# Layer norm of a Macaron pair of blocks: GpSimd's power of minus one half in two instructions of two tiles each, and VectorE's four centring instructions in two pairs

## The chip, the cores and the metric

The kernel runs on one core of a Trainium2 chip. The metric is the device time of one execution in microseconds (us), the median of several runs; lower is better. Engines are called as in the profile: PE is TensorE's matmul side and PEld its weight load, DVE is VectorE, ACT is ScalarE, POOL is GpSimd, SP is SyncE, which here only issues DMAs.

## What is computed

Eight batches of 512 tokens by 128 features go through two blocks. The first ("A") is a low-rank feed-forward, causal attention with 16 heads, and the feed-forward again; the second ("B") is a mixture of experts, linear attention with a Taylor feature map, and the mixture again. A layer norm stands ahead of each of these six, and one more inside the attention of block A.

```
def _layernorm(x, axis=-1, eps=1e-05):
    m = jnp.mean(x, axis=axis, keepdims=True)
    v = jnp.var(x, axis=axis, keepdims=True)
    return (x - m) / jnp.sqrt(v + eps)
...
    x = x + 0.5 * _L0_ffn_ref(_layernorm(x, axis=-1), L0_ffn_U1, L0_ffn_V1, L0_ffn_b1, L0_ffn_U2, L0_ffn_V2, L0_ffn_b2)
    x = x + _L0_attn_ref(_layernorm(x, axis=-1), L0_attn_Wq, L0_attn_Wk, L0_attn_Wv, L0_attn_Wo, L0_attn_gamma, L0_attn_beta)
...
    x = x + _L1_attn_ref(_layernorm(x, axis=-1), L1_attn_Wq, L1_attn_Wk, L1_attn_Wv, L1_attn_Wo)
```

That is seven layer norms for each of eight batches, 56 in all, and each is over 512 tokens: four tiles of 128 tokens (one token a partition) by 128 features.

## The kernel before

**Streams.** Two streams run side by side. In the steady part the "left" one works through block A of batch i+1 (A1) while the "right" one works through block B of batch i (B2). Each has its own half of SBUF and four PSUM banks. The tables `ORDER_A` and `ORDER_B` list the steps of a block, and strings of L and R in `LOOP` say, for each engine by itself, from which stream its next step comes. The order on every engine is thus fixed by hand: an engine whose next instruction has to wait does nothing else meanwhile. There are a beginning, a body of five turns, and a finish.

**One layer norm.** It is three steps on four engines:

- `stat` on DVE: four `bn_stats` (L879) and four `bn_aggr` (L882), one a tile, leave mean and variance in `h.mv`, and the last one raises `mv_ready`.
- `stat` on POOL (`ln_scale`, L678): it adds epsilon to the four variances (L680, 128x4), waits for that through `vare_ready`, and raises them to the power of minus one half (L682, 128x4, the exponents in `neghalf`) into `h.rstd`, which raises `rstd_ready`.
- `centre` on DVE (L885): it waits for `rstd_ready`, and four `tensor_scalar` (L890), one a tile of 128x128, subtract the mean and multiply by `rstd`. The last one raises `ln_ready`.
- `norm` or `split` on PE (L1140): it waits for `ln_ready` and transposes the four tiles (L1145) into one bank, which ACT reads out next (L731 or L735).

Between its `stat` and its `centre` DVE may have steps of the other stream, as its string has it; where it has none, it waits for POOL.

**What else POOL does.** It masks: `affine_select` (L689) on the attention weights of either stream, and for block B a `tensor_scalar` over 128x1024 or 128x512 (L709) that adds one. These are POOL's other steps, and they stand in its order between those of the layer norms.

Of the kernel before, what the change touches and what calls it, by code (L numbers as in the profile page):

```python
# [33 lines left out]
ALU = mybir.AluOpType  # L34
# [5 lines left out]
NT = S // P  # L40
# [29 lines left out]
def segment(kt, head, heads):  # L70


    if kt == 0:
        return head * S
    if kt == 1:
        return (heads + head) * S
    if kt == 3:
        return (heads + head) * S + WIDTH[1]
    return 2 * heads * S + head * WIDTH[2]
# [301 lines left out]
def build_program(nc, x, w, cst, out):  # L381
    ctx = ExitStack()
    with ctx:  # L383
        def sb(name, shape, dt=F32):
            return ctx.enter_context(nc.sbuf_tensor(name, shape, dt))
# [16 lines left out]
        neghalf = sb("neghalf", [P, NT])  # L402
# [150 lines left out]
        def run(eng, fns, engine):  # L553

            steps(fns, 0, "begin", engine)
            for i in range(TURNS):
                steps(fns, i, "body", engine)
            steps(fns, 0, "finish", engine)
# [15 lines left out]
        def drained(h, it, step, unit):  # L574

            u = h.T[step, unit]
            return it * (h.per.act if u.engine == "act" else h.per.dve) + u.count
# [86 lines left out]
        @block.gpsimd  # L664
        def _(pool):
            for h in (A1, A2):
                pool.memset(h.vaug[:, :, :, HD0:HD0 + 1], 1.0).then_inc(setup, 1)
            pool.memset(neghalf[:, :], -0.5).then_inc(setup, 1)
            pool.memset(epsilon[:, :], LN_EPS).then_inc(setup, 1)
            for k in range(GP):  # L670
                if k:
                    pool.memset(column[:, k, 0:k], 0.0)
                pool.memset(column[:, k, k + 1:32], 0.0)
                last = pool.memset(column[:, k, k:k + 1], 1.0)
            last.then_inc(setup, 1)
            pool.wait_ge(setup, SETUP)

            def ln_scale(h, it, k, step):  # L678
                pool.wait_ge(h.mv_ready, it * h.lns + k + 1)
                pool.tensor_tensor(h.vare[:, :], h.mv[:, :, 1], epsilon[:, :], ALU.add).then_inc(h.vare_ready, 1)  # L680
                pool.wait_ge(h.vare_ready, it * h.lns + k + 1)
                pool.tensor_tensor(h.rstd[:, :], h.vare[:, :], neghalf[:, :], ALU.pow).then_inc(h.rstd_ready, 1)  # L682

            def mask(buf, heads, kt, fill=0.0):

                step = {0: S, 1: S, 3: S, 2: WIDTH[2]}[kt]
                s0 = segment(kt, 0, heads)
                v = bass.AP(buf.tensor, buf.offset + s0, [list(buf.ap[0]), [step, heads], [1, P]])
                return pool.affine_select(out=v, in_=v, compare_op=ALU.is_ge, fill=fill, base=0,  # L689
                                          pattern=[[0, heads], [1, P]], channel_multiplier=-1)  # L690

            def exp(h, it, n, step):
                g, u = divmod(n, NU0)
                if u in COMPLETE0:
                    pool.wait_ge(h.act, drained(h, it, step, "s"))
                for kt in COMPLETE0.get(u, ()):
                    mask(h.probs[:, g % 2, :], GH, kt).then_inc(h.masked0, 1)

            def sq(h, it, n, step):
                p, u = divmod(n, NU1)  # L700
                if u in COMPLETE1:
                    k = p * NC + list(COMPLETE1).index(u)
                    pool.wait_ge(h.act, drained(h, it, step, "s"))
                    for kt in COMPLETE1[u]:
                        last = mask(h.wts[:, p % 2, :], 2, kt, -1.0)
                    last.then_inc(h.cut1, 1)
                    pool.wait_ge(h.cut1, it * NPAIR * NC + k + 1)
                    v = h.wts[:, p % 2, (u // 2 * 2) * S:(u + 1) * S]
                    pool.tensor_scalar(v, v, 1.0, 1.0, ALU.mult, ALU.add).then_inc(h.masked1, 1)  # L709

            run(pool, dict(stat=ln_scale, exp=exp, sq=sq), "pool")


# [118 lines left out]
        def _(dve):  # L832
            passed = Passed(dve)
# [51 lines left out]
            def centre(h, it, k, step):  # L885

                src = h.attn if h in (A1, A2) and k == 2 else h.x
                passed.wait_ge(h.rstd_ready, it * h.lns + k + 1)
                for t in range(NT):
                    last = dve.tensor_scalar(h.ln[:, t, :], src[:, t, :], h.mv[:, t, 0:1], h.rstd[:, t:t + 1],  # L890
                                             ALU.subtract, ALU.mult)
                last.then_inc(h.ln_ready, 1)
# [219 lines left out]
            def out1(h, it, n, step):  # L1112
                ps = full(passed, h, it, step, "y")
                if n:
                    passed.wait_ge(h.dve, drained(h, it, f"out1 {n - 1}", "y"))
                dve.tensor_tensor(h.x[:, :, :].rearrange("p t d -> p (t d)"), ps[:, :],
                                  h.x[:, :, :].rearrange("p t d -> p (t d)"), ALU.add).then_inc(h.dve, 1)

            fns = dict(stat=stat, centre=centre, split=split, low=low, down0=down0, qkv0=qkv0, pad0=pad0, pv0=pv0, turn=turn,
                       out0=out0, take=take, route=route, gate=gate, expert=expert, qk1=qk1, pad1=pad1, recip=recip,  # L1120
                       scale=scale, out1=out1)
# [304 lines left out]
```

## Time and profile before

| | |
|---|---|
| median of 3 runs | 1490.75 us (1488.5 to 1492.01) |
| the profiled execution | 1486.09 us |
| its span, first to last instruction | 1484.4 us |
| mean granted TensorE clock | 0.934 of full speed |
| busy share of the span: PE, DVE, ACT, POOL | 84%, 64%, 49%, 28% |
| a turn of the body | 181 us |
| layer norms: left, right | 31, 25 |

The busy shares say which engine has least room, not what the end waits for. With an order fixed by hand, what counts for an instruction is what ended the idle time before it ("idle before <- releaser"), and whether the engine behind it stood idle for it in turn.

### The profile page before, as it was taken

Reading aid. Unit: us, or ns where it says so; the run is one execution under the profiler, and the core shown is the slowest. Engines: PE = TensorE matmul, PEld = TensorE weight load, DVE = VectorE, ACT = ScalarE, POOL = GpSimd, SP = SyncE. Lnnn points to the kernel's source line nnn. Section 1 sums busy time; section 2 is a strip of 40 time slices with the busy share of each in tenths; the row PEclk is TensorE's granted clock in tenths of the full one; section 3 lists DMA queues with packets and bytes.
Section 4 is the critical chain, followed back from the end, with each engine's and each line's share of the span. In section 5 each row is a group of like instructions: output and inputs, shape, how many; then the busy total and the mean of one; then the engine's idle time right before and its main releaser. Section 6 shows DMA issues by size and latency. Waiting matters only on the chain. (4 is left out here: it accounts for less than half of the span.)

```text
span 1484.4 us, 26633 instructions
## 1 busy us (share of the span) xinstructions
PE 1242.9 (84%) x10064; PEld 705.9 (48%) x10064; DVE 950.1 (64%) x2923; ACT 725.7 (49%) x1247; POOL 417.7 (28%) x707
## 2 busy tenths in 40 slices
PE   5698668987789887899878887798878998879998
PEld 3354234444544455444554445544455445543456
DVE  6985377446974469834797347964488646874267
ACT  3165335643366433664346543465435663456533
POOL 1023101640026400264003540035300362016730
PEclk9699779998999989999999999899998999999999
DMA  3100001000010000100001000010010100011000
GB/s 117 43 2 2 8 22 34 11 8 7 23 44 2 8 13 17 44 1 9 19 11 44 1 9 22 8 44 2 8 29 1 44 2 1 13 38 44 2 2 15
DMA packets 37201, 28.75 MB, mean 19 GB/s; under 512 B 7960, under 2 KB 36304, under 8 KB 37072
## 3 DMA queue, kind: packets, MB, share of 16 engines
q1 hardware_dynamic: 37072, 27.04, 6.7%
q8 instruction: 80, 1.31, 0.4%
q14 instruction: 49, 0.40, 0.1%
HBM read 5.90 MB, written 2.10 MB: 5 GB/s over the span
## 5 line engine op out<-in xcount | busy, mean ns | idle before, releaser
L775 ACT ACTIVATE left<-bank 128x512 f32<-128x512 f32 x280 | 159.9, 598 | 86.3 <-PE bank L1237 84.5
L968 DVE TENSOR_REDUCE left<-bank 128x4 f32<-128x512 f32 x280 | 184.5, 682 | 22.6 <-PE bank L1218 21.8
L819 ACT ACTIVATE right<-bank 128x512 f32<-128x512 f32 x280 | 158.6, 598 | 82.2 <-PE bank L1324 80.1
L689 POOL TENSOR_SCALAR_AFFINE_SELECT left<-left 128x512 f32<-128x512 f32 (+1 forms) x144 | 82.5, 587 | 397.6 <-ACT left L775 382.7
L1160 PE MATMUL bank<-right,pairs 128*128 128x512 f16 x588 | 161.6, 399 | 17.3 <-DVE right L1047 10.1
L1216 PE MATMUL bank<-left 128*128 128x512 f16 (+1 forms) x448 | 123.3, 324 | 42.4 <-DVE left L968 25.9
L709 POOL TENSOR_SCALAR right<-right 128x1024 f32<-128x1024 f32 x168 | 151.9, 904 | 14.7
L689 POOL TENSOR_SCALAR_AFFINE_SELECT right<-right 128x256 f32<-128x256 f32 (+1 forms) x240 | 99.3, 426 | 133.3 <-ACT right L819 122.8
L1350 PE MATMUL bank<-right 128*32 128x256 f32 (+3 forms) x1792 | 134.6, 439 | 0.0
L1068 DVE SCALAR_TENSOR_TENSOR right<-bank,right 128x128 f32<-128x128 f32 x448 | 125.8, 343 | 11.7 <-PE bank L1300 6.4
L1300 PEld LDWEIGHTS bank<-ew,right 128*128 128x128 f32 x896 | 113.8, 191 | 25.8 <-DVE right L1057 12.5
L1300 PE MATMUL bank<-ew,right 128*128 128x128 f32 x896 | 121.0, 278 | 6.0 <-DVE right L1057 5.8
L1237 PE MATMUL bank<-left 128*128 128x512 f16 (+1 forms) x448 | 102.4, 303 | 22.1 <-DVE left L968 13.0
L794 ACT ACTIVATE right<-bank 128x512 f32<-128x512 f32 x112 | 66.2, 597 | 106.5 <-PE bank L1160 105.4
L1218 PE MATMUL bank<-negmask,identb 128*128 128x128 bf16 x512 | 103.5, 234 | 0.0
L1324 PE MATMUL bank<-right 96*128 96x512 f16 x448 | 96.9, 304 | 4.9 <-ACT right L819 1.9
L680 POOL TENSOR_TENSOR right<-right,epsilon 128x4 f32<-128x4 f32 x25 | 5.3, 213 | 332.6 <-DVE right L882 332.6
L1160 PEld LDWEIGHTS bank<-right,pairs 128*128 128x128 f16 x588 | 52.8, 101 | 78.7 <-DVE right L1047 18.0
L1350 PEld LDWEIGHTS bank<-right 128*32 128x32 f32 x1792 | 54.4, 110 | 65.7 <-issue 62.5
L1216 PEld LDWEIGHTS bank<-left 128*128 128x128 f16 x448 | 46.2, 103 | 81.8 <-DVE left L968 30.6
L1337 PE MATMUL bank<-right,column 128*32 128x256 f32 (+3 forms) x896 | 75.7, 447 | 1.2 <-POOL right L709 1.1
L985 DVE COPY left<-bank 128x512 f32<-128x512 f32 x28 | 19.4, 691 | 87.8 <-PE bank L1248 87.8
(274 smaller groups left out, 2201.8 us busy)
## 6 DMA issues: line engine op xcount, KB each, us to landing
right<-right SPq DMA_DIRECT2D x168, 64.0 KB, 2.0
left<-left SPq DMA_DIRECT2D x168, 32.0 KB, 1.8
left<-x_dram SPq DMA_DIRECT2D x7, 256.0 KB, 2.6
out_dram<-right SPq DMA_DIRECT2D x7, 256.0 KB, 2.2
left<-left SPq DMA_DIRECT2D x24, 64.0 KB, 2.0
right<-right SPq DMA_DIRECT2D x24, 32.0 KB, 1.9
wo<-wo_dram SPq DMA_DIRECT2D x1, 512.0 KB, 3.7
ew<-ew_dram SPq DMA_DIRECT2D x1, 512.0 KB, 4.6
```

What stands on the lines that cost most here:

```text
L689: return pool.affine_select(out=v, in_=v, compare_op=ALU.is_ge, fill=fill, base=0, pattern=[[0, heads], [1, P]], channel_multiplier=-1)
L709: pool.tensor_scalar(v, v, 1.0, 1.0, ALU.mult, ALU.add).then_inc(h.masked1, 1)
L775: act.activation(h.probs[:, g % 2, u * S:(u + 1) * S], ps[:, :], ACT.Exp).then_inc(h.act, 1)
L819: act.activation(h.wts[:, p % 2, u * S:(u + 1) * S], ps[:, :], ACT.Square, bias=1.0, scale=FEAT ** -0.5).then_inc(h.act, 1)
L968: dve.tensor_reduce(h.bmax[:, u * NT:(u + 1) * NT], ps[:, :].rearrange("p (b k) -> p b k", k=P), AX.X, ALU.max).then_inc(h.dve, 1)
L1068: last = dve.scalar_tensor_tensor(out=dst[:, t, :], in0=ps[:, t * P:(t + 1) * P], scalar=h.comb[:, t, e:e + 1], in1=h.acc[:, t, :], op0=AL ...
L1160: done = mm(out, left, right, start=first, stop=last)
L1216: mm(ps[:, c0:c0 + n_keys], h.q0a[:, g, qt * P:(qt + 1) * P], h.kpad0[:, g * GH + j, 0:n_keys], start=True, stop=False)
L1218: last = mm(ps[:, c0 + n_keys - P:c0 + n_keys], identb[:, :], negmask[:, :], start=False, stop=True)
L1237: last = mm(ps[:, c0:c0 + WIDTH[kt]], h.kpad0[:, g * GH + j, kt * P:(kt + 1) * P], h.q0a[:, g, kt * P:S], start=True, stop=True)
L1300: last = mm(ps[:, t * P:(t + 1) * P], h.hexp[:, e % 2, t * P:(t + 1) * P], ew2[:, e, :], start=True, stop=True)
L1350: last = mm(h.num[HD1 * j + c:HD1 * j + c + 32, kt * P:S], h.v1[:, kt, hd * HD1 + c:hd * HD1 + c + 32], h.wts[:, p % 2, c0:c0 + WIDTH[kt]] ...
```

## The change

POOL's one power instruction over four columns becomes two over two columns each, and each raises `rstd_ready`, which now counts two for a layer norm. On DVE the wait for `rstd_ready` moves inside the loop: the first two tiles wait for the first power, and the other two for the second. What is computed stays the same, and so do all tables of the order.

```
@@ ln_scale, POOL
                 pool.wait_ge(h.vare_ready, it * h.lns + k + 1)
-                pool.tensor_tensor(h.rstd[:, :], h.vare[:, :], neghalf[:, :], ALU.pow).then_inc(h.rstd_ready, 1)
+                for t in range(0, NT, 2):
+                    pool.tensor_tensor(h.rstd[:, t:t + 2], h.vare[:, t:t + 2], neghalf[:, t:t + 2], ALU.pow)\
+                        .then_inc(h.rstd_ready, 1)
@@ centre, DVE
                 src = h.attn if h in (A1, A2) and k == 2 else h.x
-                passed.wait_ge(h.rstd_ready, it * h.lns + k + 1)
                 for t in range(NT):
+                    passed.wait_ge(h.rstd_ready, (it * h.lns + k) * 2 + t // 2 + 1)
                     last = dve.tensor_scalar(h.ln[:, t, :], src[:, t, :], h.mv[:, t, 0:1], h.rstd[:, t:t + 1],
                                              ALU.subtract, ALU.mult)
                 last.then_inc(h.ln_ready, 1)
```

On POOL, in a turn of the body, at the fourth layer norm of block A (left), with block B's masks (right) behind it, before:

```order
L680 TENSOR_TENSOR left<-left,epsilon 128x4 [waits mv_ready_A1]
L682 TENSOR_TENSOR left<-left,neghalf 128x4 [waits vare_ready_A1]
L689 AFFINE_SELECT right<-right 128x2x128 [waits act_B2]
L709 TENSOR_SCALAR right<-right 128x1024 [waits cut1_B2]
L689 AFFINE_SELECT right<-right 128x2x128 [waits act_B2]
```

and after, with every line number behind L682 higher by two:

```order
L680 TENSOR_TENSOR left<-left,epsilon 128x4 [waits mv_ready_A1]
L683 TENSOR_TENSOR left<-left,neghalf 128x2 [waits vare_ready_A1]
L683 TENSOR_TENSOR left<-left,neghalf 128x2
L691 AFFINE_SELECT right<-right 128x2x128 [waits act_B2]
L711 TENSOR_SCALAR right<-right 128x1024 [waits cut1_B2]
```

The second power stands between the first and the masks, and waits for nothing.

On DVE, in a turn of the body, at the last layer norm of block B (right), which ends in `centre` right behind its own `stat`, before:

```order
L882 BN_AGGR right<-right 128x2 [waits dve_step_B2]
L882 BN_AGGR right<-right 128x2 x3
L890 TENSOR_SCALAR right<-right 128x128 [waits rstd_ready_B2]
L890 TENSOR_SCALAR right<-right 128x128 x3
L919 SCALAR_TENSOR_TENSOR left<-bank1,left 128x512 [waits filled_A1]
```

and after:

```order
L884 BN_AGGR right<-right 128x2 [waits dve_step_B2]
L884 BN_AGGR right<-right 128x2 x3
L892 TENSOR_SCALAR right<-right 128x128 [waits rstd_ready_B2]
L892 TENSOR_SCALAR right<-right 128x128
L892 TENSOR_SCALAR right<-right 128x128 [waits rstd_ready_B2]
L892 TENSOR_SCALAR right<-right 128x128
L921 SCALAR_TENSOR_TENSOR left<-bank1,left 128x512 [waits filled_A1]
```

The third centring instruction has a wait of its own; nothing has changed places.

## Rows read from the trace of the kernel before

**Rows 1.** The page: busy time, share of the span and instructions of each engine.
```profile
PE 1242.9 (84%) x10064; PEld 705.9 (48%) x10064; DVE 950.1 (64%) x2923; ACT 725.7 (49%) x1247; POOL 417.7 (28%) x707
```

**Rows 2.** Waits of the whole span: us in total, times, longest us.
```profile
PEld bank L1145 <- DVE left L890: 39.8, 27, 6.1
...
PEld bank L1145 <- DVE right L890: 31.6, 22, 4.6
...
DVE left L890 <- POOL left L682: 20.8, 18, 2.7
...
DVE right L890 <- POOL right L682: 14.2, 16, 1.4
```

**Rows 3.** POOL's groups by shape: times, busy us, mean ns of one, idle before.
```profile
L689 POOL TENSOR_SCALAR_AFFINE_SELECT right<-right 128x256 f32<-128x256 f32 x224 | 89.3, 410 | 122.9 <-ACT right L819 122.8
L689 POOL TENSOR_SCALAR_AFFINE_SELECT left<-left 128x512 f32<-128x512 f32 x112 | 69.7, 637 | 382.8 <-ACT left L775 382.7
...
L682 POOL TENSOR_TENSOR left<-left,neghalf 128x4 f32<-128x4 f32 x31 | 31.3, 1009 | 2.4
L682 POOL TENSOR_TENSOR right<-right,neghalf 128x4 f32<-128x4 f32 x25 | 25.2, 1008 | 2.0
...
L680 POOL TENSOR_TENSOR left<-left,epsilon 128x4 f32<-128x4 f32 x31 | 6.2, 199 | 153.1 <-DVE left L882 153.1
```

**Rows 4.** Timeline of POOL and DVE (start us, us), right layer norm at 529 us.
```profile
529.05 0.20 POOL L680 TENSOR_TENSOR right<-right,epsilon 128x4 f32<-128x4 f32 x1 [13.64 <-DVE right L882]
529.33 1.01 POOL L682 TENSOR_TENSOR right<-right,neghalf 128x4 f32<-128x4 f32 x1
...
530.38 1.11 DVE L890 TENSOR_SCALAR right<-right 128x128 f32<-128x128 f32 x4 [1.40 <-POOL right L682]
...
531.55 1.12 PE L1145 MATMUL bank<-ident,right 128*128 128x128 f32 x4 [0.36 <-DVE right L890]
```

**Rows 5.** Timeline of POOL and DVE, left layer norm at 491 us, with masks behind.
```profile
491.27 1.01 POOL L682 TENSOR_TENSOR left<-left,neghalf 128x4 f32<-128x4 f32 x1
492.25 0.41 POOL L689 TENSOR_SCALAR_AFFINE_SELECT right<-right 128x256 f32<-128x256 f32 x1
492.75 1.04 POOL L709 TENSOR_SCALAR right<-right 128x1024 f32<-128x1024 f32 x1
...
492.32 2.27 DVE L890 TENSOR_SCALAR left<-left 128x128 f32<-128x128 f32 x4 [0.22 <-POOL left L682]
```

**Rows 6.** Timeline of POOL and DVE: two powers and what DVE ran beside them.
```profile
296.85 1.01 POOL L682 TENSOR_TENSOR left<-left,neghalf 128x4 f32<-128x4 f32 x1
...
297.12 0.18 DVE L1097 COPY dlateB<-right 64x48 f32<-64x48 f32 x1
...
1111.84 1.01 POOL L682 TENSOR_TENSOR right<-right,neghalf 128x4 f32<-128x4 f32 x1
...
1111.88 1.14 DVE L958 TENSOR_SCALAR left<-left,headmask 96x512 f16<-96x512 f16 x4
```

**Rows 7.** Timeline of DVE and PE, right layer norm at 567 us.
```profile
567.86 1.01 POOL L682 TENSOR_TENSOR right<-right,neghalf 128x4 f32<-128x4 f32 x1
...
569.19 1.11 DVE L890 TENSOR_SCALAR right<-right 128x128 f32<-128x128 f32 x4
...
570.36 0.90 PE L1145 MATMUL bank<-ident,right 128*128 128x128 f32 x3 [1.40 <-DVE right L890]
```

**Rows 8.** Two lines' instructions (min/median/max ns), and who waited for L709.
```profile
L890 DVE TENSOR_SCALAR right<-right x100: 334/341/1061, 11.9 to 1456.8; 128x128 f32<-128x128 f32 x100
...
L1097 DVE COPY dlateB<-right x14: 183/183/516, 297.1 to 1442.2; 64x48 f32<-64x48 f32 x14
...
  PEld bank L1337: 12.3, 17
  PE bank L1337: 1.1, 5
```

**Rows 9.** Windows of one turn each: busy us of PE, PEld, DVE, ACT, POOL; granted clock.
```profile
524.00:705.00 181.00, 154.00 (x1258) 87.87 (x1258) 116.17 (x363) 91.48 (x156) 52.10 (x86) 0.94 0.06 17
```

More of the change, by code:

```diff
@@ L681, in ln_scale @@
                 pool.wait_ge(h.vare_ready, it * h.lns + k + 1)
-                pool.tensor_tensor(h.rstd[:, :], h.vare[:, :], neghalf[:, :], ALU.pow).then_inc(h.rstd_ready, 1)
+                for t in range(0, NT, 2):
+                    pool.tensor_tensor(h.rstd[:, t:t + 2], h.vare[:, t:t + 2], neghalf[:, t:t + 2], ALU.pow)\
+                        .then_inc(h.rstd_ready, 1)
             def mask(buf, heads, kt, fill=0.0):
@@ L887, in centre @@
                 src = h.attn if h in (A1, A2) and k == 2 else h.x
-                passed.wait_ge(h.rstd_ready, it * h.lns + k + 1)
                 for t in range(NT):
+                    passed.wait_ge(h.rstd_ready, (it * h.lns + k) * 2 + t // 2 + 1)
                     last = dve.tensor_scalar(h.ln[:, t, :], src[:, t, :], h.mv[:, t, 0:1], h.rstd[:, t:t + 1],
```

## Prediction

> **What bounds the kernel now.** I read the page first: PE is busy 84% of the span, DVE 64%, POOL 28% [rows 1], so PE has least room. It still stands idle for some 240 us, and with a fixed order each of those gaps is on the path unless something makes it up later. The view of waits then says where. Ahead of the transposes of the layer norms (L1145) PE's weight load sat idle 39.8 us on the left and 31.6 us on the right, 49 times in all, until DVE's centring (L890) was done [rows 2]. One step back, DVE itself waited for POOL's power (L682) 18 times on the left and 16 on the right, 35.0 us together [rows 2]. So 34 of the 56 layer norms have the chain statistics, POOL, DVE, PE with nothing of the other stream to hide POOL. In the other 22 DVE is busy elsewhere when the power comes: at 567 us it starts centring 0.32 us after the power has ended [rows 7].
>
> The timeline of one of the 34 gives the lengths [rows 4]: the power starts at 529.33 and takes 1.01 us; centring starts at 530.38, 0.04 after its end, and takes 1.11 us for four tiles; PE transposes at once. From the start of the power, which I call 0, the centring ends at 2.16 us. One centring instruction takes 0.34 us [rows 8], so the others follow at (1.11 - 0.34) / 3 = 0.26 us, and a pair takes 0.60.
>
> **What the change does, part by part.**
>
> *The power over two columns.* The trace has only the one over four, 1.01 us [rows 3]. From below it costs 0.51 (half, no fixed part), from above 1.01 (nothing depends on the columns). The nearest row is the addition on the same engine with the same shape and as many inputs: 0.20 us [rows 3]. What the power takes beyond it, 0.81 us for four columns, I put down to computing column by column, and half of that is 0.40: I take 0.60 us. The masks, 0.41 us for 256 columns and 0.64 for 512 [rows 3], also have a fixed part of 0.18 and grow with the rest. This is the term on which everything hangs.
>
> *The second power.* It waits for nothing, and POOL starts such a follower 0.03 us before the end of the one ahead (a power runs from 491.27 to 492.28, and the mask behind it starts at 492.25 [rows 5]). So it ends at 0.60 - 0.03 + 0.60 = 1.17 us.
>
> *Centring.* The first pair starts at 0.64 and ends at 1.24. The third instruction is due at 0.64 + 0.52 = 1.16 by DVE and at 1.17 + 0.04 = 1.21 by POOL; POOL is late. The second pair ends at 1.81. That is 0.35 us ahead of 2.16; I count 0.34. In general the end is twice the price of the power plus 0.61, so the break-even is at (2.16 - 0.61) / 2 = 0.78 us a power: 0.51 would give 0.5 us, 1.01 would cost 0.47.
>
> *Where it counts.* I went through the 34 in the timeline. In four PE comes to the transposes later than the centring for reasons of its own (the first of all, the second of the right stream, two at 1203 and 1214 us), and in two PE is idle for 0.05 us or less ahead of them. That leaves 28, with PE idle ahead of them for 0.3 us at the least in all but one (0.36 in rows 4), so the gain is not cut off: 28 x 0.34 = 9.5 us. In seven of the 28 the centring now meets POOL's masks: at 492.32 it takes 2.27 instead of 1.11 us, since L709 runs from 492.75 to 493.79 and two of the four come to lie behind it [rows 5]. Pulled forward by 0.3 us, one more tile gets through ahead of L709; it is worth about 0.1 us beyond the 0.34 (PE's idle time ahead of the transposes is the limit), another 0.6 us. Together 10.1 us.
>
> *Where it does not.* At the other 22 the pairs find both powers done: in rows 7 the third instruction is due 0.32 + 0.52 = 0.84 us after the first power's end of now, and the second power ends 0.16 us behind that of now. They cost nothing at 0.60 us a power. With the power at 1.01 that cover is gone for five of them, by 0.15 us each.
>
> *What POOL pays.* 56 x 0.2 = 11 us more busy time, on an engine that is idle for seven tenths of the span [rows 1]. Queued behind the second power are masks, 0.16 us later than now, and PE waits for them: 17 weight loads, 12.3 us, and 5 matmuls, 1.1 us, over the whole run [rows 8]. At most two a turn stand close behind a power, so this is under 1 us, and I leave it in the rounding below. The waits that DVE gains are for a semaphore that is up or about to be; queued behind them are the other stream's steps, and these come sooner too, since the last tile is sooner.
>
> *How much arrives.* An engine that was idle and starts 0.34 us earlier passes that on until it meets a wait that was not moved: a DMA, a bank of the other stream. I take three quarters, a choice, between half and all: 10.1 x 0.75 = 7.6 us. The profiled execution would go from 1486.1 to 1478.5 us. It is itself 4.7 us below the median of the runs, 1490.75, so the median goes to **1483.2 us**.
>
> **Does DVE run beside the power?** This decides whether the first pair moves at all. The centring is an instruction that POOL can block: beside L709 one was held for the whole of it (the 2.27 us of rows 5, and a longest of 1061 ns against a median of 341 [rows 8]). Beside a power the trace shows something else. A copy of the kind that L709 stretches (183 ns as a rule, 516 at most [rows 8]) starts 0.27 us into a power and takes 0.18 us; four `tensor_scalar` start 0.04 us after a power's start, end with the last one beyond the power's end, and take 1.14 us together, while the power takes its 1.01 [rows 6]. Neither side was held. So I take the centring beside the second power at its own price.
>
> The Trainium skill ("SBUF — State Buffer", section "Who interferes with whom") speaks against the change here: a VectorE `tensor_scalar` in its two-port mode and a GpSimd instruction share a pair of ports, and whichever issues first holds it for its whole length while the other is fully blocked. The masks agree with it (2.27 us for 1.11); the two powers of rows 6 do not. By it the first pair would be held until the second power ends, and the time would be that of rival 2.
>
> **The rivals.**
>
> 1. *The power has a fixed price.* If two columns cost what four do, 1.01 us, the last tile ends at 2.63 instead of 2.16. It is slower from 0.78 us on. All 34 pay 0.47 (PE, which now waits, waits longer), and the five of rows 7's kind 0.15: 16.7 us. Four fifths of it arrive, 13.4 us, since a loss on a waiting engine is made up less: 1504 us. For it: only one shape of the power is in the trace, and POOL's duration there is the same to 1% each time. Against it: the addition of the same shape shows that reading, writing and starting cost 0.20. Chance 0.14.
> 2. *The lock.* The first pair is held until the second power's end at 1.17. The one that waits ends about 0.1 us behind it, the other three 0.26 apart: 1.17 + 0.1 + 0.77 = 2.04, still 0.12 ahead of now. 28 x 0.12 x 0.75 = 2.5 us: 1488 us. Against it stand rows 6. Chance 0.06. The reverse, in which the first pair holds the second power until 1.24, ends at 1.24 + 0.60 + 0.04 + 0.60 = 2.48 and costs 34 x 0.32 x 0.8 = 8.7 us: 1499 us, 0.04; against it, POOL has started the second power before DVE hears of the first.
> 3. *In between, or lost on the way.* The power costs 0.7 to 0.85 us, or the gain of a layer norm is taken back at the next wait of the same turn (PE idles 27 us of each 181 [rows 9], so there are many). 1488 to 1494 us, taken as 1490. Chance 0.13.
>
> **How the numbers follow.** The forecast has 0.63. Its own span is 1478 to 1488: the low end is a power of 0.51 us (28 x 0.42, PE's idle time the limit, nearly all arriving), the high end 0.7 us with half arriving. TensorE's clock adds to both ends. Over a turn the granted clock is 0.94 [rows 9], so some 22 of 181 us are at 1.2 GHz, at a price of at most 11 us a turn; if shorter waits move a tenth of that, five turns move by some 4 us either way, and I give 2 to the low end. The range takes in the forecast, rival 3 and the lock, and leaves out rival 1 and the reverse: **1476 to 1495 us**. About 0.2%, 3 us, is what a measurement of this kernel can tell from no change. Faster by more than that: 0.65, nearly all of the forecast and a little of rivals 2 and 3. Within it: 0.16. Slower: 0.19, rival 1, the reverse and a sliver of rival 3.
>
> **What would show it.** In the changed kernel's profile: the two-column power at about 600 ns, 112 times, in place of 1009; in the layer norms of rows 4's kind a first pair that starts 0.64 us after the power and a second about 0.57 us behind it; DVE's idle time ahead of the first centring down from 1.40 to about 1.0 us, and 34 short new waits ahead of the third; a turn of the body about 1 us under 181. A power near 1.0 us would prove rival 1, a first centring instruction of 0.6 us and more in places with no mask near would prove the lock, and a second power well over 0.6 us its reverse. If the local gain is there and the turn is not shorter, the three quarters were wrong.

## The result, and the profile after

| | before | after |
|---|---|---|
| median of 20 runs each | 1488.5 us (1481.9 to 1496.5) | 1483.6 us (1477.2 to 1486.5) |
| ratio, with its 95% interval | | 0.9963 (0.995 to 0.9977) |
| span of the profiled execution | 1484.4 us | 1482.1 us |
| mean granted TensorE clock, mean of the runs | 0.928 | 0.928 |

By the ratio the change takes 0.37% off, 5.5 us, between 3.4 and 7.4; the two medians lie 4.9 us apart. The forecast was 1483.2 us, 7.6 us (0.51%) faster. It moved the right way by three quarters of what was forecast, but the parts behind that number came out differently. The median of before over 20 runs is 2.2 us below the one over 3 that the prediction started from, which is why the two absolute times agree better than the two differences: that the time measured is within 0.4 us of the forecast is luck. (The clock given for before is the mean of the 92 runs of it beside the experiments; for these 20 none is recorded.)

The line that answers to the power in [rows 3], from the view of that source line (columns: times, min/median/max ns, first and last start):

```profile
L683 POOL TENSOR_TENSOR left<-left,neghalf x62: 688/690/736, 10.2 to 1423.1; 128x2 f32<-128x2 f32 x62
L683 POOL TENSOR_TENSOR right<-right,neghalf x50: 688/690/807, 8.6 to 1453.5; 128x2 f32<-128x2 f32 x50
```

Two columns take 0.69 us, not 0.60. Four take 1.01, so the power has a fixed part of 0.37 us and 0.16 us a column. The timeline that answers to [rows 4], the right layer norm of the same turn:

```profile
527.12 0.20 POOL L680 TENSOR_TENSOR right<-right,epsilon 128x4 f32<-128x4 f32 x1 [13.32 <-DVE right L884]
527.40 1.36 POOL L683 TENSOR_TENSOR right<-right,neghalf 128x2 f32<-128x2 f32 x2
...
528.12 1.28 DVE L892 TENSOR_SCALAR right<-right 128x128 f32<-128x128 f32 x4 [1.08 <-POOL right L683]
...
529.46 0.69 PE L1147 MATMUL bank<-ident,right 128*128 128x128 f32 x2 [0.28 <-DVE right L892]
```

From the start of the power, the first pair starts at 0.72 us (before: all four at 1.05), the second power ends at 1.36, and the last tile is done at 2.00 instead of 2.16. DVE's wait is 1.08 us instead of 1.40, but the four centrings now spread over 1.28 instead of 1.11 us, since the third stands 0.16 us for its power. A layer norm of this kind gains 0.16 us, less than half of the 0.34 forecast.

The timeline that answers to [rows 5], with the masks behind it:

```profile
489.67 1.36 POOL L683 TENSOR_TENSOR left<-left,neghalf 128x2 f32<-128x2 f32 x2
490.98 0.41 POOL L691 TENSOR_SCALAR_AFFINE_SELECT right<-right 128x256 f32<-128x256 f32 x1
491.48 1.04 POOL L711 TENSOR_SCALAR right<-right 128x1024 f32<-128x1024 f32 x1
...
490.40 2.20 DVE L892 TENSOR_SCALAR left<-left 128x128 f32<-128x128 f32 x4
```

Here the last tile is done 2.93 us after the power's start instead of 3.32: 0.39 us sooner. POOL's masks come 0.33 us later in this chain and centring starts 0.32 us sooner, so that three tiles get through and the fourth is held (1.21 us), where before the second was. The eight places of this kind are not alike: 0.39 us sooner at four of them, 0.14 to 0.20 at three, and 1.27 at one, where the fourth tile too gets through.

The waits that answer to [rows 2] (us in total, times, longest us):

```profile
PEld bank L1147 <- DVE left L892: 35.2, 26, 6.0
...
PEld bank L1147 <- DVE right L892: 29.6, 20, 4.5
...
DVE left L892 <- POOL left L683: 15.4, 14, 2.7
```

PE's weight load lost 6.6 us of its 71.4 us of waiting for centring. Taken over the 49 layer norms whose transposes start within 0.2 us of the last centring's end before, the time from the last `bn_aggr` to the last centring is 6.3 us shorter in sum than before, where the prediction had 10.1.

One place has got worse. In the body, the layer norm inside the attention has no wait of DVE for the power, only POOL's masks behind it. DVE there before:

```profile
480.32 0.23 DVE L1101 CAST rsplitB<-right 64x64 bf16<-64x64 f32 x1
480.59 0.30 DVE L1102 TENSOR_TENSOR right<-right,rsplitB 64x64 f32<-64x64 f32 x1
480.92 1.11 DVE L1103 CAST rsplitB<-right 64x64 bf16<-64x64 f32 x1
```

and after, with POOL's row beside it:

```profile
478.45 0.49 DVE L1103 CAST rsplitB<-right 64x64 bf16<-64x64 f32 x1
478.98 0.30 DVE L1104 TENSOR_TENSOR right<-right,rsplitB 64x64 f32<-64x64 f32 x1
479.31 1.11 DVE L1105 CAST rsplitB<-right 64x64 bf16<-64x64 f32 x1
...
477.13 1.34 POOL L683 TENSOR_TENSOR left<-left,neghalf 128x2 f32<-128x2 f32 x2
478.44 0.77 POOL L691 TENSOR_SCALAR_AFFINE_SELECT right<-right 128x256 f32<-128x256 f32 x2
479.29 1.04 POOL L711 TENSOR_SCALAR right<-right 128x1024 f32<-128x1024 f32 x1
```

These are the reciprocals of block B, for which PE waits. The first cast now falls beside a mask (0.49 us, not 0.23), and the second still starts beside L711 and is held for its whole length. From DVE's first transpose of this chain to its last it takes 4.90 us, 4.64 before, in four of the five turns; in the first turn it takes 4.89 instead of 5.26.

### The profile page after: what moved, and what is told of

It is laid out like the page before. It is cut to its first block and busy times, and to the rows that moved or that the text cites. A ratio compares the mean times of both kernels' runs of the same rounds, so it can differ in the third digit from the quotient of the medians.

```text
span 1482.1 us, 26689 instructions
## 1 busy us (share of the span) xinstructions
PE 1246.6 (84%) x10064; PEld 709.3 (48%) x10064; DVE 950.7 (64%) x2923; ACT 725.7 (49%) x1247; POOL 436.5 (29%) x763
## 5 line engine op out<-in xcount | busy, mean ns | idle before, releaser
L711 POOL TENSOR_SCALAR right<-right 128x1024 f32<-128x1024 f32 x168 | 151.7, 903 | 14.7
```

## The experiments

All ratios are to the kernel before, run on the same chip in the same rounds; the experiments ran on four chips, so across them only the ratios are compared, and gains and losses in us are worked out from the ratios.

**What the first three were to tell apart.** *Theory 1*: the power costs 0.37 us and 0.16 a column, nothing holds anything else, and what a layer norm's chain gains or loses arrives. *Theory 2*: such steps are mostly made up later. *Theory 3*: the power has a floor. And the lock: centring is held beside a power.

`e1_four`, four powers of one column:

```
-                for t in range(0, NT, 2):
-                    pool.tensor_tensor(h.rstd[:, t:t + 2], h.vare[:, t:t + 2], neghalf[:, t:t + 2], ALU.pow)\
+                for t in range(NT):
+                    pool.tensor_tensor(h.rstd[:, t:t + 1], h.vare[:, t:t + 1], neghalf[:, t:t + 1], ALU.pow)\
...
-                    passed.wait_ge(h.rstd_ready, (it * h.lns + k) * 2 + t // 2 + 1)
+                    passed.wait_ge(h.rstd_ready, (it * h.lns + k) * NT + t + 1)
```

> The power in four instructions of one column each, each centring instruction waiting for its own. The two prices known, 1.01 us for four columns and 0.69 for two, lie on a line of 0.37 + 0.16 a column. Theory 1 (a fixed part and a part by the column, and what a layer norm loses or gains arrives nearly in full): one column takes 0.53 us, the fourth ends at 2.1 us after the first's start, the last tile at 2.46 instead of 2.16 of before, so 0.30 x 28 to 34 = 8 to 10 us slower than before, ratio 1.006. Theory 2 (such losses and gains are mostly made up at later waits, and the 5 us measured for the change have another source): the same 0.53 us, but a ratio under 1.003. Theory 3 (a floor near 0.69, whatever the columns): the last tile ends at 3.1 us, 27 us or more slower, ratio 1.018 and over.

Measured: 1509.4 us, ratio 1.0128 (1.0086 to 1.0171), mean clock 0.910. One column takes 0.55 us. Timeline of the second left layer norm:

```profile
31.83 2.09 POOL L683 TENSOR_TENSOR left<-left,neghalf 128x1 f32<-128x1 f32 x4
...
32.41 0.34 DVE L892 TENSOR_SCALAR left<-left 128x128 f32<-128x128 f32 x1 [0.94 <-POOL left L683]
32.93 0.35 DVE L892 TENSOR_SCALAR left<-left 128x128 f32<-128x128 f32 x1 [0.17 <-POOL left L683]
33.44 0.34 DVE L892 TENSOR_SCALAR left<-left 128x128 f32<-128x128 f32 x1 [0.17 <-POOL left L683]
33.96 0.35 DVE L892 TENSOR_SCALAR left<-left 128x128 f32<-128x128 f32 x1 [0.17 <-POOL left L683]
```

The last tile is done 2.48 us after the first power's start (expected 2.46). The price by the column holds at three sizes, and theory 3 is out. Every centring instruction here takes its ordinary 0.34 us while the next power runs beside it: the power doesn't hold centring, so the lock is out as well. But the kernel lost 19 us (13 to 25) where 8 to 10 were expected, and its own profile explains less still. The chains of the 49 layer norms are 3.9 us longer in sum (8.5 us longer, less 4.7 us that seven of them gain where centring now gets by POOL's masks), and the reciprocals, held by no mask, take 3.58 us instead of 4.64.

`e2_both`, the change's two powers, with the first tile waiting for both:

```
-                    passed.wait_ge(h.rstd_ready, (it * h.lns + k) * 2 + t // 2 + 1)
+                    passed.wait_ge(h.rstd_ready, (it * h.lns + k) * 2 + 2)
```

> The two powers of the change, but the first tile too waits for both: the price without the cover. Theory 1: the last tile ends at 1.37 + 0.04 + 1.11 = 2.52 us instead of 2.16, so 0.36 x 34 = 12 us slower than before if all of it arrives, ratio 1.006 to 1.009; the cover is then worth 0.5 us a layer norm. Theory 2: ratio under 1.004. A theory by which the centring beside the second power is held by it would give the same time as for the change itself, ratio 0.996.

Measured: 1505.0 us, ratio 1.0108 (1.0072 to 1.0144), clock 0.916. Splitting the power without the cover (centring the first pair beside the second power) costs 16 us (11 to 21), and the cover is worth 22. The chains of the 49 layer norms are 10.1 us longer in sum, so more arrives than goes in: about one and a half times. Theory 2 is out.

`e6_no_eps`, the change without the addition of epsilon, which is then missing from the result:

```
-                pool.tensor_tensor(h.vare[:, :], h.mv[:, :, 1], epsilon[:, :], ALU.add).then_inc(h.vare_ready, 1)
-                pool.wait_ge(h.vare_ready, it * h.lns + k + 1)
                 for t in range(0, NT, 2):
-                    pool.tensor_tensor(h.rstd[:, t:t + 2], h.vare[:, t:t + 2], neghalf[:, t:t + 2], ALU.pow)\
+                    pool.tensor_tensor(h.rstd[:, t:t + 2], h.mv[:, t:t + 2, 1], neghalf[:, t:t + 2], ALU.pow)\
...
```

> The change with the addition of epsilon (and the wait for it) left out: the power reads the variances themselves, so epsilon is missing from the result. It takes 0.28 us more out of the same chain, with no other engine touched. Theory 1: the last tile ends 0.16 + 0.28 = 0.44 us sooner than before, 28 x 0.4 = 11 us at full arrival, ratio 0.991 to 0.994. Theory 2: ratio 0.996, as for the change.

Measured: 1461.8 us, ratio 0.9824 (0.979 to 0.9858), clock 0.943. The chains are 17.0 us shorter in sum, the kernel 26. Again one and a half times, now on the side of the gain. Against the change, 0.28 us less at each layer norm (10.7 us less of the 49 chains) are worth 21 us: the kernel does wait for this chain.

**Is POOL's longer time free?** `e7_pool_load`: the kernel before, with one power more behind each layer norm's own, which nobody reads or waits for.

```
                 pool.tensor_tensor(h.rstd[:, :], h.vare[:, :], neghalf[:, :], ALU.pow).then_inc(h.rstd_ready, 1)
+                pool.tensor_tensor(spare[:, 0:2], epsilon[:, 0:2], neghalf[:, 0:2], ALU.pow)
```

> The kernel before, with one more power over two columns behind each layer norm's own, from constants into a spare tile that nobody reads: 0.66 us more of GpSimd's time at 56 places, nobody waiting for it, only the masks behind it later. The change itself adds 0.36 us at each. Theory 1 (POOL's longer time costs next to nothing): within 0.1% of before, 0 to 1.5 us. Theory 4 (the masks behind it, or VectorE's instructions that meet them, take back a part of the gain): 3 us or more slower, ratio 1.002 and over.

Measured: 1482.7 us, ratio 0.9966 (0.9944 to 0.9987). Neither theory: useless work on POOL made the kernel 5 us *faster*, about as much as the change. The profile differs from before at two places a turn. The first is the reciprocals again:

```profile
477.15 1.01 POOL L683 TENSOR_TENSOR left<-left,neghalf 128x4 f32<-128x4 f32 x1
478.12 0.70 POOL L684 TENSOR_TENSOR spare<-epsilon,neghalf 128x2 f32<-128x2 f32 x1
478.79 0.80 POOL L691 TENSOR_SCALAR_AFFINE_SELECT right<-right 128x256 f32<-128x256 f32 x2
479.68 1.05 POOL L711 TENSOR_SCALAR right<-right 128x1024 f32<-128x1024 f32 x1
...
478.98 0.33 DVE L1105 CAST rsplitB<-right 64x64 bf16<-64x64 f32 x1
...
480.53 0.39 PE L1361 MATMUL bank<-right,spread 128*128 128x512 bf16 x1 [1.42 <-DVE right L1107]
```

The masks come 0.65 us later, so L711 starts behind the second cast, which takes 0.33 us and not 1.11. The whole chain takes 3.77 us instead of 4.64, and PE's wait for it is 1.42 us; before it was 2.29:

```profile
483.25 0.39 PE L1359 MATMUL bank<-right,spread 128*128 128x512 bf16 x1 [2.29 <-DVE right L1105]
```

The second is the fourth layer norm of block A, that of [rows 5]: the masks come behind all four tiles there, and centring takes 1.2 us instead of 2.27. That makes the chain about 1.06 us shorter a turn, 6.7 us over seven layer norms.

So the question became where the change's own 5.5 us come from: the shorter chain, or the masks that it moves. `e8_spare_one` has the spare power at that place alone (`if h in (A1, A2) and k == 2`), `e9_spare_rest` everywhere else.

> The kernel before with the spare power only behind the layer norm inside the attention (the third of block A), 8 places of 56. With it at all 56 the kernel was 0.34% faster, and its trace differs from before at one place a turn: behind this layer norm POOL's masks come 0.65 us later, and VectorE's cast and subtraction in the reciprocals of block B no longer fall beside the mask's 1.04 us (0.33 instead of 1.11 us). Theory A (the whole 5 us come from that place): the same as with all 56, ratio 0.995 to 0.998. Theory B (they come from POOL's later masks in general, or from chance): within 0.1% of before.

> The complement: the spare power behind all layer norms but those of the attention. Theory A: no change, ratio 0.999 to 1.001 (POOL's extra time costs nothing there). Theory B: 0.997, as with all 56.

Measured: 1481.7 us, ratio 0.9961 (0.994 to 0.9982), and 1485.2 us, ratio 0.999 (0.9962 to 1.0019). The gain sits at the eight layer norms inside the attention, of which five (one a turn) have the reciprocals beside their masks; the 48 others show no change clear of noise. The interval of the second is wide, but its middle is where theory A has it. It says one thing more: `e9_spare_rest` keeps the 6.7 us that centring gains on the masks at the fourth layer norm, and the kernel is 1.5 us faster (5.7 faster to 2.8 slower). PE was idle for only 0.37 to 0.48 us ahead of the transposes at four of those seven, so most of the 1.06 us can't reach it there.

Then the change in the same two parts, with one power of four columns where it isn't applied:

```
-                for t in range(0, NT, 2):
+                width = 2 if not (h in (A1, A2) and k == 2) else NT
+                for t in range(0, NT, width):
...
```

The power of four columns raises `rstd_ready` by two at once, so DVE's waits stay as in the change.

> The change at all layer norms but the one inside the attention, which keeps its single power of four columns. VectorE never waits for the power there, so the local gain of 0.16 us has nothing to do with that place; what the change does there is only to move POOL's masks by 0.35 us. Theory 1 (the change gains by the shorter chain at the layer norms where VectorE waits): as the whole change, ratio 0.995 to 0.998. Theory 5 (it gains, like the spare power, by moving the masks at that one place): no change, 0.999 to 1.001.

> The complement: two powers only at the layer norm inside the attention, 8 of 56 places. Theory 1: within 0.1% of before. Theory 5: ratio 0.996, as for the whole change.

Measured: without that place 1477.9 us, ratio **0.9932** (0.9907 to 0.9956); there alone 1491.3 us, ratio 1.0021 (0.9995 to 1.0047). Theory 5 is out. (At two of the eight places, both outside the body, VectorE does wait for the power, 1.4 us each in the kernel before.) The two powers gain 10 us at the 48 layer norms, and it isn't the masks behind them: `e9_spare_rest` moves the masks at the same 48 by more and has 0.999, and the two intervals don't meet. The two ratios here together make 0.9953, the whole change measured 0.9963. Of the two, only the gain is clear of noise by itself; that the place inside the attention costs something is also what 0.9932 against 0.9963 says, whose intervals overlap by 0.0006. That it does so through the reciprocals is not shown. They take 4.64 us in the profile of `e12_not_k2`, as before, and 4.90 in that of the change; but `e13_k2_only` has the same two powers at that place, and they take 4.64 there too:

```profile
483.12 1.37 POOL L684 TENSOR_TENSOR left<-left,neghalf 128x2 f32<-128x2 f32 x2
484.45 0.84 POOL L692 TENSOR_SCALAR_AFFINE_SELECT right<-right 128x256 f32<-128x256 f32 x2
485.38 1.04 POOL L712 TENSOR_SCALAR right<-right 128x1024 f32<-128x1024 f32 x1
...
484.44 0.23 DVE L1104 CAST rsplitB<-right 64x64 bf16<-64x64 f32 x1
...
485.04 0.34 DVE L1106 CAST rsplitB<-right 64x64 bf16<-64x64 f32 x1
485.42 1.15 DVE L1107 TENSOR_TENSOR rsplitB<-right,rsplitB 64x64 bf16<-64x64 f32 x1
```

Here the first cast starts 0.01 us ahead of the mask and takes its ordinary time, and the instruction behind the second cast is the one held. In the change the mask starts 0.01 to 0.02 us ahead of the cast, in all five turns, and the cast takes 0.49 us. Over the whole run the reciprocals of the change are some 1 us longer than before, those of `e13_k2_only` 0.4 us shorter.

**Do the two gains add up?** `e10_both_edits` is the whole change plus the spare power inside the attention, `e15_best` the change without that place plus the spare power there:

```
+                width = 2 if not (h in (A1, A2) and k == 2) else NT
+                for t in range(0, NT, width):
...
+                if h in (A1, A2) and k == 2:
+                    pool.tensor_tensor(spare[:, 0:2], epsilon[:, 0:2], neghalf[:, 0:2], ALU.pow)
```

> The changed kernel with the spare power behind the layer norm inside the attention alone. In the changed kernel the second power moves the mask there by 0.35 us, too little: its cast still takes 1.11 us. Theory A: the two gains add up, 5.5 + 5 us, ratio 0.992 to 0.994. If instead the change's own gain of 0.37% is in truth only this displacement of the masks, the ratio stays at 0.996.

> The change at all layer norms but the one inside the attention; there one power of four columns as before, and behind it the spare power over two columns, which holds POOL's masks back by 0.65 us. By the two runs that had one of these parts each (0.9932 and 0.9961), if they add up: ratio 0.988 to 0.991, some 15 us faster than before and faster than any kernel so far that computes all of it. If both gains come out of the same slack of the turn: 0.992 to 0.994. At the place itself the reciprocals should take 3.8 instead of 4.6 us from VectorE's first transpose to its last.

Measured: 1480.3 us, ratio 0.9956 (0.9938 to 0.9973), and 1479.3 us, ratio 0.9923 (0.9895 to 0.995). The first is hardly more than the change, the second hardly more than `e12_not_k2`. What may have become of the second gain shows in the profile of `e10_both_edits`:

```profile
479.17 0.77 POOL L694 TENSOR_SCALAR_AFFINE_SELECT right<-right 128x256 f32<-128x256 f32 x2
480.03 1.04 POOL L714 TENSOR_SCALAR right<-right 128x1024 f32<-128x1024 f32 x1
...
480.40 2.07 DVE L895 TENSOR_SCALAR left<-left 128x128 f32<-128x128 f32 x4
...
482.53 0.66 PE L1150 MATMUL bank<-ident,left 128*128 128x128 f32 x4 [1.38 <-DVE left L895]
```

The masks are out of the way of the reciprocals (3.70 us) and stand in that of the centring right behind them, which takes 2.07 us instead of 1.08. From the first transpose to the last centring it is 5.70 us there, 5.64 in the kernel before, 5.90 in the change and 5.28 in `e7_pool_load`. In `e15_best`, where it should have been as in `e7_pool_load`, it is 5.31 to 5.45 us. That would account for `e10_both_edits`, though no run isolates it; for `e15_best` the interval reaches from no further gain to the sum of both, and it stays open. `e12_not_k2` needs no spare work, so it is the version I would keep: 9 to 10 us faster than before and, if the intervals are read at their middles, 4 to 5 us faster than the change.

**Epsilon on VectorE**, `e14_eps_dve`:

```
@@ stat, DVE
-                last.then_inc(h.mv_ready, 1)
+                last.then_inc(h.vare_ready, 1)
+                passed.wait_ge(h.vare_ready, it * h.lns + k + 1)
+                dve.tensor_scalar(h.vare[:, :], h.mv[:, :, 1], LN_EPS, None, ALU.add).then_inc(h.mv_ready, 1)
...
```

POOL's addition and its wait for `vare_ready` are left out.

> The changed kernel with the addition of epsilon on VectorE instead of GpSimd: 0.04 us of its own wait and 0.17 us of work there, and 0.07 us until GpSimd starts its power, so the power starts 0.28 us after the statistics instead of 0.36. Theory 1, by what leaving the addition out gave (0.28 us less of chain, 21 us less of time): 0.08 us is worth 3 to 6 us, less what VectorE's 0.2 us cost at the 22 layer norms where it has other work (up to 4 us): ratio 0.992 to 0.996. Theory 2 (small steps in this chain are noise): 0.996 to 0.998.

Measured: 1483.9 us, ratio 0.9968 (0.9943 to 0.9994): the same as the change. The 0.08 us are there: at the tenth layer norm of the right stream (that of [rows 4]) the time from the last `bn_aggr` to the last centring is 2.29 us, 2.36 in the change and 2.52 before. What takes them back is not shown; the interval doesn't shut out theory 1 (0.992 to 0.996). Making the power itself on VectorE was not tried.

**What arrives of what goes in.** These are the chains of the 49 layer norms (last `bn_aggr` to last centring) against before, from one profile each, seven of them where centring meets POOL's 128x1024 mask and the 42 others; and the kernel's time. All in us, minus is shorter:

| | 7 with masks | 42 others | kernel, with its interval |
|---|---|---|---|
| `e1_four` | -4.7 | +8.5 | +19 (13 to 25) |
| `e2_both` | +0.7 | +9.4 | +16 (11 to 21) |
| the change | -2.9 | -3.4 | -5.5 (-7.4 to -3.4) |
| `e6_no_eps` | -6.6 | -10.4 | -26 (-31 to -21) |
| `e12_not_k2` | -3.6 | -4.5 | -10 (-14 to -6) |
| `e14_eps_dve` | -4.8 | -3.2 | -5 (-8 to -1) |
| `e9_spare_rest` | -6.7 | -0.5 | -1.5 (-5.7 to +2.8) |
| `e7_pool_load` | -6.7 | -2.4 | -5 (-8 to -2) |
| `e8_spare_one` | +0.2 | -2.4 | -6 (-9 to -3) |
| `e10_both_edits` | -1.5 | -4.4 | -6.5 (-9 to -4) |
| `e13_k2_only` | +0.1 | +1.0 | +3 (-1 to +7) |
| `e15_best` | -3.3 | -5.0 | -11.5 (-16 to -7) |

The kernel follows the 42 others, at 1.5 to 2.5 times their sum wherever it moved clear of noise, and hardly the seven. The sum of all 49 is a poor guide: it has 7.2 us gained for `e9_spare_rest` and 6.3 for the change, 3.9 lost for `e1_four` and 10.1 for `e2_both`, and the kernel has both pairs the other way round.

Where so much more than the chain comes from is open. One candidate is the clock. In the runs with the largest effects it goes along (0.943 without epsilon, 0.916 and 0.910 in the two slower kernels), but not in the others: 0.928 in the change and 0.929 in `e12_not_k2`, against 0.928 before. Within the kernel before itself, 92 runs of it, a run with 0.01 more of mean clock is 6.6 us shorter (correlation -0.92). By that slope the clock would carry 10 of the 26 us of `e6_no_eps`, 8 of the 16 of `e2_both` and 12 of the 19 of `e1_four`, but nothing of the change's 5.5; and within the change's own 20 runs the slope is 2.4 us (correlation -0.54). `e11_filler` tried it: six matmuls on the identity ahead of PE's wait at the second layer norm of each block, on the changed kernel.

```
-                passed.wait_ge(h.ln_ready, it * h.lns + k + 1)
                 ps = fill(passed, h, it, step, "lnT")
+                if k == 1:
+                    for j in range(6):
+                        mm(ps[:, 0:P], ident[:, :], ident[:, :], start=True, stop=True)
+                passed.wait_ge(h.ln_ready, it * h.lns + k + 1)
```

> The changed kernel with six matmuls of 128x128 on the identity, into the bank that the transposes then overwrite, issued ahead of PE's wait for the centring at the second layer norm of every block, where PE is idle 1.4 to 1.8 us: work of no use, inside idle time. Theory C (a good part of what a layer norm gains or loses comes from the granted clock, which drops after PE has been idle): the clock rises from 0.928 to 0.935 or more and the kernel gets 3 us or more faster than the change, ratio 0.991 to 0.994. Theory D (idle time counts only as itself; clock and time merely go together): the clock and the time stay, ratio 0.996 to 0.998, or up to 3 us slower where the six don't end in time.

Measured: 1481.9 us, ratio 0.9963 (0.9948 to 0.9978), clock 0.9345. The clock rose by 0.007, and the time stayed that of the change; the slope of the kernel before would have given 4 to 5 us. So a higher mean clock is not by itself a shorter kernel. The test is not clean, though. In the left stream the six lie inside idle time. In the right stream PE has only 0.2 to 0.4 us there, and the six end late:

```profile
419.96 1.56 PE L1147 MATMUL bank<-ident 128*128 128x128 f32 x12
421.36 0.60 PE L1150 MATMUL bank<-ident,right 128*128 128x128 f32 x4
421.94 0.60 PE L1231 MATMUL bank<-ident,left 128*4 128x128 f32 x4
```

Centring had ended at 420.28 there, so these transposes are 1.1 us late. That the next group then starts without a wait (in the change it waits 0.95 us) says that most of this was slack anyway. Over all 56 layer norms the transposes start 12 us later behind their statistics than in the change, and what that cost is not known. Whether clock and time move together because waiting lowers the clock, or the clock's own lapses also lengthen the time, stays open.

## Why the prediction came out right, and where its steps were off

- *PE has least room, and the chain statistics, POOL, centring, transposes is what it waits for.* Right: 0.28 us more taken out of it at each layer norm were worth 21 us (`e6_no_eps`), and the same two powers without the earlier start of centring cost 16 us (`e2_both`).
- *The power over two columns, 0.60 us.* This is the term that was mis-sized. It was built as the addition's 0.20 us plus half of the remaining 0.81. The fixed part of the power is 0.37 us, not 0.20: the addition of the same shape was the wrong measure for it, and why the power's is larger no run shows. Measured 0.69, within the two ends of 0.51 and 1.01 and under the break-even of 0.78 that was worked out.
- *The gain of one layer norm, 0.34 us.* 0.16 us for that reason. The formula (twice the power plus 0.61) gives 1.99 for the end, and 2.00 was measured.
- *Masks at seven places, 0.44 us each.* In the mean about right (0.41 us over eight), but one by one from 0.14 to 1.27 us; and by `e9_spare_rest` little of what is gained there reaches the end.
- *28 places, 10.1 us together.* 6.3 us in the profile. With 0.69 us in the prediction's own sum it would be 28 x 0.16 + 0.6 = 5.1 us, so the shortfall is the price of the power.
- *Three quarters arrive.* In the change 5.5 of 6.3 us, nearly nine tenths, with an interval from half to more than all, so this run alone doesn't refute it. But there is no such share. Of the chains without masks one and a half to two and a half times their sum arrives, of those with masks little, and the prediction, which made one list of both and allowed for no more than all of it, had no step for that. The smaller local gain and the larger share made up for each other, and that the total came out close to the forecast is luck.
- *The 22 layer norms without a wait cost nothing, and POOL's longer time under 1 us.* Not shown for the 22 layer norms as a whole, and wrong for the masks at one kind of place. The prediction looked at who waits for the masks and not at which DVE instructions run beside them, though it had the price in [rows 5]. Five layer norms a run, one a turn, have masks behind the power and the reciprocals beside them. Moving the masks by 0.33 us lengthened that chain by 0.26 in four turns of the change and left it as it was in `e13_k2_only`; moving them by 0.65 us shortened it by 0.87, and the kernel by 6 us (`e8_spare_one`). What the place costs in the whole change is not clear of noise.
- *DVE runs beside the power undisturbed.* Right; in `e1_four` each centring took 0.34 us beside a power. The rule of the Trainium skill ("SBUF — State Buffer", section "Who interferes with whom"), that the pair of ports is held for the whole instruction, is borne out by the masks (1.11 us of cast beside L711) and not by the power, beside which centring took its 0.34 us. Whether the power holds the ports for a part of its time only, no run shows.
- *The rivals.* A fixed price of 1.01 us, the lock and its reverse are out by the first profile. Rival 3, a power of 0.7 to 0.85 us with the gain lost on the way, was nearly right as to the price (0.69 us), and wrong as to what follows from it: 1490 us was taken, 1483.6 measured.

## What to carry to other kernels

Splitting an instruction pays only if its fixed part is small against what the consumer can start early, so fit that part at two sizes before splitting: here 0.69 against 1.01 us left 0.16 of a hoped 0.34 us. Where two engines hold each other up, an edit also moves everything queued behind it; look for the instructions that run beside that, and try the edit only where the consumer really waits (leaving out 8 of 56 places gave 0.9932 for 0.9963, two intervals that just touch). And test an edit's gain against the same displacement without its purpose: useless work at one layer norm of seven gave as much as the whole change. Adding up what each place gains is not enough either: the same 1 us counted for more than itself at one kind of layer norm and for almost nothing at another.

## What the runs showed of the hardware that I had not expected

- GpSimd's power on 128 partitions takes 0.55, 0.69 and 1.01 us for 1, 2 and 4 columns, 0.37 to 0.39 of it fixed. A second one starts 0.03 to 0.04 us before the first has ended.
- A VectorE cast of 64x64 takes 0.23 us alone and 1.11 beside a GpSimd `tensor_scalar` of 128x1024. Where two start together, a hundredth of a microsecond decides: a cast takes 0.49 us where the `affine_select` starts 0.01 to 0.02 us ahead of it (the change), and 0.23 where the cast starts 0.01 us ahead (`e13_k2_only`), in all five turns of either. The `tensor_scalar` of 128x1024 also held a DVE `tensor_tensor` of 64x64 for 1.15 us, 0.38 otherwise.
- The same program's runs differ by up to 1.3% (1479.7 to 1499.6 us over 92 runs of the kernel before), and the mean granted clock goes with them: 6.6 us for 0.01. With a dozen runs against 34 the interval is 3 us to either side.
